# A pre-norm block of splat attention and a gated feed-forward layer: the order of the prologue, of the side work and of the stage loads

## What is computed

```python
x = x + attn(layernorm(x)); x = x + ffn(layernorm(x))
# attn: 16 heads, 16 splats per head, 16 dimensions per head
q, k, v = split(x @ qkv_w.T)
q_weights = exp(sum((q - centers) ** 2) * inv_var)      # per token, head, splat
k_weights = exp(sum((k - centers) ** 2) * inv_var)
logits = einsum('bihs,bjhs,hs->bijh', q_weights, k_weights, amplitudes)
out = softmax(logits / temp, axis=2) @ v ; return out @ out_w.T
# ffn: token shift and gate, x_prev is x moved by one token
xr = mu_r * x + (1 - mu_r) * x_prev ; xk = mu_k * x + (1 - mu_k) * x_prev
return sigmoid(xr @ W_r.T) * (square(relu(xk @ W_k.T)) @ W_v.T)
```

## Time and profile before

| what | us |
|---|---|
| median of 3 runs | 2332.38 (2332.07 to 2335.14) |
| the profiled execution, its own time | 2329.31 |
| its span in the trace | 2327.5 |
| PE busy in the span | 2189.1 (94%) |
| ACT busy in the span | 2003.1 (86%) |
| DVE busy in the span | 907.5 (39%) |
| granted PE clock, mean | 0.984 |

### The profile page before, as it was taken

The page is one execution under the profiler, slowest core; times in us unless marked ns, Lnnn a source line. Parts: engine busy times, 40 slices in busy tenths (PEclk is TensorE's granted clock), DMA queues, the critical chain, the costliest instruction groups (busy, mean ns, idle before and its releaser), DMA issues.

```text
span 2327.5 us, 46042 instructions
## 1 busy us (share of the span) xinstructions
PE 2189.1 (94%) x19886; PEld 902.2 (39%) x19886; DVE 907.5 (39%) x1777; ACT 2003.1 (86%) x2160; POOL 278.4 (12%) x260
## 2 busy tenths in 40 slices
PE   6689999999999899999999999999999999999997
PEld 3233333433443344334444343443433333333344
DVE  4223344334435243452533445244343342323426
ACT  2478999999999799898989999898999999998883
POOL 0112122211110110111102011110200000000000
PEclk9889999999999999999999999999999999999999
DMA  4632425226051421431542243421243131310111
GB/s 131 169 84 87 98 89 119 85 74 155 22 125 56 84 72 47 85 99 37 121 92 82 64 85 99 88 71 45 77 106 76 36 65 47 49 46 17 40 39 35
DMA packets 165582, 180.27 MB, mean 77 GB/s; under 512 B 82832, under 2 KB 108816, under 8 KB 162480
## 3 DMA queue, kind: packets, MB, share of 16 engines
q1 hardware_dynamic: 163264, 177.01, 30.2%
q10 hardware_dynamic: 2096, 0.14, 0.1%
HBM read 86.45 MB, written 75.89 MB: 70 GB/s over the span
## 4 chain that ended last, share of the span: by engine, by line
PE 74%; ACT 16%; DVE 4%; SPq 2%; DMA 2%; issue 1%; ACTq 0%; DVEq 0%
PE ps_pv L700 35%; PE ps_scores L683 21%; ACT probs L1007 14%; PE ps_step L728 13%; PE ps_step L745 2%; PE ps_scores L718 1%; ACT weight L1067 1%; PE ps_scores L713 1%; DVE den_all L1432 1%; SPq L638 1%; DVE o_raw L1317 1%; SPq L510 1%; DMA q_parts<-parts 0%; DMA attn<-attn_kept 0%; DVE mixed_r L1300 0%
## 5 line engine op out<-in xcount | busy, mean ns | idle before, releaser
L1007 ACT ACTIVATE probs<-ps_scores 128x1024 f32<-128x1024 f32 x2048 | 1932.4, 1032 | 226.4 <-PE ps_scores L683 218.8
L700 PE MATMUL ps_pv<-probs,vals 128*32 128x512 f32 x8192 | 1089.5, 616 | 15.4 <-DVE o_raw L1317 12.2
L683 PE MATMUL ps_scores<-q_aug,k_aug 49*128 49x512 f32 x4096 | 722.8, 441 | 42.8 <-ACT probs L1007 36.5
L683 PEld LDWEIGHTS ps_scores<-q_aug,k_aug 49*128 49x128 f32 x4096 | 336.7, 185 | 595.9 <-ACT probs L1007 470.0
L700 PEld LDWEIGHTS ps_pv<-probs,vals 128*32 128x32 f32 x8192 | 255.1, 144 | 347.7 <-issue 277.0
L1124 POOL TENSOR_TENSOR packed<-qk 32x512 f32<-32x512 f32 x224 | 244.7, 1092 | 946.6 <-DVE qk L1250 933.4
L1432 DVE RECIPROCAL den_all<-den_all 128x512 f32<-128x512 f32 x63 | 210.8, 3346 | 0.7
L1129 POOL TENSOR_TENSOR k_act<-k_act 128x512 f32<-128x512 f32 x28 | 30.7, 1096 | 1015.5 <-DVE k_act L1253 1015.5
L1317 DVE COPY o_raw<-ps_pv 128x512 f32<-128x512 f32 x64 | 44.2, 691 | 240.7 <-PE ps_pv L700 240.7
L1250 DVE COPY qk<-ps_step 128x512 f32<-128x512 f32 x56 | 38.7, 691 | 220.4 <-PE ps_step L728 220.4
L1228 DVE TENSOR_SCALAR weight<-ps_step,cen_sq 128x512 f32<-128x512 f32 x57 | 42.8, 750 | 174.6 <-PE ps_step L745 174.5
(11 more groups left out here) (201 smaller groups left out, 1044.5 us busy)
## 6 DMA issues: line engine op xcount, KB each, us to landing
q_aug<-q_parts SPq DMA_DIRECT2D x128, 192.0 KB
k_aug<-k_parts SPq DMA_DIRECT2D x30, 768.0 KB, 10.6
k_parts<-parts SPq DMA_DIRECT2D x32, 512.0 KB, 3.0
q_parts<-parts SPq DMA_DIRECT2D x32, 512.0 KB, 2.8
packed<-qk SPq DMA_DIRECT2D x224, 64.0 KB, 2.0
x_ffn<-x SPq DMA_DIRECT2D x18, 512.0 KB, 4.3
v_kept<-v_rows SPq DMA_DIRECT2D x64, 128.0 KB, 2.4
k_parts<-parts SPq DMA_DIRECT2D x32, 256.0 KB, 3.5
```

The costliest lines, as they stand in the source:

```text
L683: mm = pe.matmul(ps_scores[:, g % RING, e, :], k_aug[rows, s % 2, pair, kt * P:(kt + 1) * P], q_aug[rows, u % 2, pair, :], start=True, sto ...
L700: mm = pe.matmul(ps_pv[32 * c:32 * c + 32, :], vals[:, s % 2, kt, :, c], probs[:, tick % PROB_SLOTS, c, :], start=(kt == 0), stop=(kt == K ...
L1007: act.activation(probs[:, tick % PROB_SLOTS, 2 * pair:2 * pair + 2, :], ps_scores[:, g % RING, :, :], ACT.Exp).then_inc(probs_ready, 1)
```

## The change

The order of work changes; no product, activation or transfer of the steady part is dropped, except that each exponential of weights becomes two, one for each side.

- Prologue: ACT copies tile 0's transposes before it waits for the constants. `q1` is projected before PE waits for the flag, and PE reads the flag only at the end. Values use `v_rows` and `gate` in turn, each with a semaphore. SP stores a tile's values first, then loads the parts and values of the tile before.
- PE's loop: in an odd gap the pieces stand ahead of its one tick of values. An even gap is as before.
- ACT's loop goes by gaps. The weights' exponential is taken per side (128x512), in the first gap of the next four that holds work (`full`), else in the first; the splits and stores follow that.
- `stage_tick` moves a stage's loads out of the nine ticks from an attention load's tick on.
- Two mixing operations that fell on the tick before a unit's end move behind `take`.

```diff
 FIRST = (..., "k1", "value10", "value11",
-         "dist_k0", "dist_q0", "q1", "turn20", "turn21", "k2", ...
+         "q1", "dist_k0", "dist_q0", "turn20", "turn21", "k2", ...
...
+WEIGHED_AFTER = 4
+def gap_of(tick):
+    return next(gap for gap in itertools.count() if name_of(gap) == tick)
+def full(gap):
+    work = PIECES_AT.get(name_of(gap), ())
+    return sum(not name.startswith("turn") for _, name, _ in work) >= (3 if gap % 2 else 1)
+def weigh_gap(task, half, side):
+    first = gap_of(end(task, f"dist_{'kq'[side]}{half}")) + 1
+    if side:
+        first = max(first, weigh_gap(task, half, 0) + 1)
+    return next((gap for gap in range(first, first + WEIGHED_AFTER) if full(gap)), first)
+def split_tick(task, half, side):
+    return name_of(weigh_gap(task, half, side) + 2)
...
 def stage_tick(b, s):
...
-        tick = max([tick] + [end(weighed(b, s, i)[0], f"dist_q{s // 2}") + 10 for i in range(NC)])
+        tick = max([tick] + [split_tick(*weighed(b, s, i), 1) + 4 for i in range(NC)])
...
+    last = KT * FIRST_UNIT[b, s] - 12
+    tick = next((t for t in range(tick, last) if not any(t <= begin(task, "out0") - 5 < t + 9 for task in FFNS)), tick)
...
+def later(tick):
+    return tick + 1 if tick % KT == KT - 2 else tick
...
-DIST_AT = beside((end(task, f"dist_q{half}"), (task, half)) for task, half in WEIGHTS)
+WEIGH_AT = beside((weigh_gap(task, half, side), (task, half, side)) for task, half in WEIGHTS for side in range(2))
+SPLIT_AT = beside((split_tick(task, half, side), (task, half, side)) for task, half in WEIGHTS for side in range(2))
+PARTS_AT = beside((split_tick(task, half, 1) + 2, (task, half)) for task, half in WEIGHTS)
...
-MIX_AT = beside((end(task, "turn1") + (1, 1, 2, 3)[part], (task, part)) ...
-GATE_AT = beside((end(task, name) + 2, (task, name)) ...
+MIX_AT = beside((later(end(task, "turn1") + (1, 1, 2, 3)[part]), (task, part)) ...
+GATE_AT = beside((gap_of(end(task, name)), (task, name)) ...
...
+        first_v = [v_rows, gate]
...
-            for i in range(NC):
-                sp.wait_ge(first_copied, copies_before(f"value{i}1") + 1)
-                store_v(0, i)
+            for i in range(NC + 1):
+                if i < NC:
+                    sp.wait_ge(first_copied, copies_before(f"value{i}1") + 1)
+                    store_v(0, i, first_v[i % 2], first_v_stored[i % 2])
                 if i == 0:
                     sp.wait_ge(setup_dve, SETUP_SHIFT)
                     store_shifts(0, 0)
-                sp.wait_ge(v_stored, 16 * STAGES * (i + 1))
-                load_v(0, 0, TT * i, TT)
-                store_parts(0, i, 0, 2 * i)
-                sp.wait_ge(parts_stored, PARTS * 2 * (i + 1))
-                load_k(0, 0, slice(i * CHUNK, (i + 1) * CHUNK))
-                if i == 0:
-                    sp.wait_ge(shifts_stored, 16)
-                    load_q(0, q_loaded[0])
+                if i:
+                    sp.wait_ge(parts_stored, PARTS * 2 * i)
+                    load_k(0, 0, slice((i - 1) * CHUNK, i * CHUNK))
+                    if i == 1:
+                        sp.wait_ge(shifts_stored, 16)
+                        load_q(0, q_loaded[0])
+                    sp.wait_ge(first_v_stored[(i - 1) % 2], 16 * STAGES * ((i + 1) // 2))
+                    load_v(0, 0, TT * (i - 1), TT)
+                if i < NC:
+                    store_parts(0, i, 0, 2 * i)
...
+            first_project("q", 1)
             pe.wait_ge(setup_dve, SETUP_STEPS)
-            unsafe = pe.value_load(flag[0:1, 0:1], min_val=0, max_val=1)
             first_distance("k", 0)
             first_distance("q", 0)
-            first_project("q", 1)
...
                 ticks = values_in(gap)
-                for tick in ticks[:1]:
+                for tick in ticks[:-1]:
                     values(tick)
                 for task, name, part in PIECES_AT.get(name_of(gap), ()):
...
-                for tick in ticks[1:]:
+                for tick in ticks[-1:]:
                     values(tick)
...
             def first_values(i):
-                if i:
-                    act.wait_ge(v_stored, 16 * STAGES * i)
+                if i >= 2:
+                    act.wait_ge(first_v_stored[i % 2], 16 * STAGES * (i // 2))
...
+            first_turned(0)
             act.wait_ge(consts_loaded, 16 * N_CONSTS)
...
-            first_turned(0)
...
+            for gap in range(GAPS):
+                for g in range(3 * gap, min(3 * gap + 3, 2 * TICKS)):
+                    exponentials(g)
...
+                for task, half, side in WEIGH_AT.get(gap, ()):
+                    act.wait_ge(step_free, STEP_NO[task, f"dist_{'kq'[side]}{half}"] + 1)
+                    act.activation(weight[:, side, :], weight[:, side, :], ACT.Exp, scale=inv_var[:, half:half + 1]).then_inc(weighted, 1)
```

More of the change, by code:

```diff
@@ L242, in queries_tick @@
     if which:
-        tick = max(tick, end(which[0], f"dist_q{which[1]}") + 9)
+        tick = max(tick, split_tick(*which, 1) + 3)
     assert tick < KT * u - 5, (u, tick)
@@ L601, in _ @@
                     store_attn(u)
-                for task, half in DIST_AT.get(tick - 7, ()):
+                for task, half in PARTS_AT.get(tick, ()):
                     store_parts(task[1], task[2], half, PARTS_BEFORE[task, half])
@@ L1060, in _ @@
             first_weights(3)
-            for tick in range(EVENT_TICKS):
-                if tick < TICKS:
-                    exponentials(2 * tick)
-                for task, half in DIST_AT.get(tick - 4, ()):
-                    act.wait_ge(step_free, STEP_NO[task, f"dist_q{half}"] + 1)
-                    act.activation(weight[:, :, :], weight[:, :, :], ACT.Exp, scale=inv_var[:, half:half + 1]).then_inc(weighted, 1)
-                if tick < TICKS:
-                    exponentials(2 * tick + 1)
-                for task, name in GATE_AT.get(tick, ()):
+            for gap in range(GAPS):
+                for g in range(3 * gap, min(3 * gap + 3, 2 * TICKS)):
+                    exponentials(g)
+                for task, name in GATE_AT.get(gap, ()):
                     two = slice(2 * int(name[1]), 2 * int(name[1]) + 2)
@@ L1450, in _ @@
                     layernorm("ffn", n, x_ffn[:, n % 2, :, :], h_ffn, ffn_ln, part)
-                for task, half in DIST_AT.get(tick - 5, ()):
-                    late_split(task, half, 0)
-                for task, half in DIST_AT.get(tick - 6, ()):
-                    late_split(task, half, 1)
+                for task, half, side in SPLIT_AT.get(tick, ()):
+                    late_split(task, half, side)
             u = UNITS - 1
```

26 lines of the change are left out of this document (16 added, 10 removed).

## The result

The changed kernel takes 2279.97 us (median of 4 runs, 2277.29 to 2282.12), the kernel before 2333.03 in the same session (4 runs). The ratio is 0.9773, 95% interval 0.9761 to 0.9786: faster by 53 us. The forecast was 2282, range 2264 to 2303. The profiled execution took 2282.12 us, its span is 2280.3 (before: 2329.31 and 2327.5).

The account below looks back on a forecast made before the run. PE's order was taken to set the time (PE busy 94%, ACT 86%). The terms summed to -50.1 us against the profiled 2329.3, giving 2279.2; the median counterpart, 3.1 higher, was 2282, range 2264 to 2303.

Parts of the forecast that it names:

- three signs of being wrong: Stop for `packed` ending past 112 us, odd gaps staying at 3.21 us, or PE's waits for DVE passing 20 us.
- Term 1: Prologue and first stop: PE's restart moves with SP's earlier entry into the loop; -15.6 us.
- Term 2: Loop, attention loads: issuing them ahead of the stage's loads removes PE's two stops and the half clock after; -15.5 us.
- Term 3: PE's odd gaps: pieces ahead of values shorten a full gap from 3.21 to 3.14 us; -11 us.
- Term 4: ACT's weights' exponentials by sides: two of three places where PE idled and fell to half clock go; -6 us.
- Term 5: DVE's queue: earlier splits and two mixing operations behind `take` save 1 us each in some four places; -4 us.
- term 6: Odd gaps: values no longer cover a first piece's wait, and `take` has only the scores as cover; +2 us.
- The rival in which it moves on to something waited for: SP's hold behind stage loads falls on something waited for; attention loads gain 0, total 2298 us; chance 0.08.
- all boundaries cost alike: PE's odd gaps: order of scores, pieces and values is worth nothing, total 2293 us; chance 0.15.
- The slower rival: Steps starting in odd gaps wait uncovered for DVE or DMA; 2406 us if all 135 wait; chance 0.03.

## Why the prediction was right

The total came within 2 us of the median, and that is in part luck, as the terms show. None of the three signs of being wrong appeared, though one was near: the stop ended at 111.31 us (wrong past 112, forecast 107.5), odd gaps went to 3.18, and PE's waits for DVE from 125 to 2200 us were 14.6 us. By its terms (against the profiled executions):

| term | forecast | measured | from |
|---|---|---|---|
| 1 prologue and stop | -15.6 | -12.0 | restart |
| 2 attention loads | -15.5 | -15.6 | the two pairs |
| 3 pieces ahead of values | -11 | -8.2 | put back, in the trace (9.7 without the pair at 1539 us) |
| 4 exponentials by sides | -6 | -12 | put back: 10.2 + 2.2; 11.8 beside term 3, from gap 14 |
| 5 DVE's queue | -4 | at most -1.5 of its own | what is left |
| 6 lost cover | +2 | +0.5 | a wait of 0.51 us for `gate_in`, pair at 889 us |
| tail | none | +4.6 | same code |

Errors of both signs cancelled. The account by stretches closes: 12.0 to the restart, 2.7 to gap 14 (term 4's first pair and its neighbours), then 15.6 for the attention loads, 20.0 for terms 3 and 4 together and 1.5 for the rest, less 4.6 in the tail, are 47.2.

**Term 1** had the mechanism right, that the restart moves with SP's entry and not with PE's start. The head gained 4.6 us where I said 4.0, `k3` and the third split stood within 0.8 us of what I walked, the third landing at 73.14 (said 73.6). The step that failed is the fourth tile's: "only the split, issue and landing remain: 6.9 us, so 80.5". It landed at 83.52, 3.0 us late, and both parts of the way grew. From the split at 73.03 to the end of the last issue are 5.0 us, against 3.8 for the third tile before, and from there to the landing 5.5 us, against 3.0 before and with SP's old order. And "the change alters none of these rows" was 1 us off: entry to restart is 19.1 us, not 18.05. The stop did not shrink to 13 us, since PE's first scores came as early as forecast and the restart did not. The claim that the second buffer and SP's order each do their part was not tested by the walk: the runs show that either does nearly all.

**Term 2** is right in size and kind; the held issue moved to a store with slack, as the written order said. The rival in which it moves on to something waited for falls.

**Term 3** had the sign right and the size too large. The failing step is "0.89 + 1.28 + 0.97 = 3.14": the pieces take 1.32 from their start to the values', so the way from pieces to values costs 0.04 too, and the gain is 0.03 a gap and not 0.07. The count was too small in turn, as gaps with fewer pieces gain as much. The Trainium skill (TensorE: Matmul & The Clock Gate, Part 3: Packing small matmuls) says that a weight load overlaps matmuls in flight only where the row groups differ; that all boundaries cost alike was what I made of it, and it would have given nothing. The run that puts the order back is 8 us slower. Nor does the trace agree with the Trainium skill's statement: in the odd gap above the values' first weights load at 431.40 us, 0.2 us ahead of the first values at 431.61 and just as the last four instructions of the pieces start, and both kinds use all 128 rows (timeline of PE's weight loads):

```profile
431.40 0.37 PEld L742 LDWEIGHTS ps_pv<-probs,vals 128*32 128x32 f32 x8
```

The first weights of a block of scores load only as it starts, and so do those of the pieces behind scores. Both orders have one boundary with such an early load in an odd gap, so this doesn't tell why they differ by 0.03 us; that stays open.

**Term 4** was too small by half. "12 pairs stood in gaps with four pieces per pair already and cost nothing there" was the wrong step: eight of these pairs lasted 6.68 to 6.76 us in the trace of before, where a full pair lasts 6.42, and last 6.40 to 6.43 now; I had looked only at pairs with a stop. The other part had the mechanism right: the pairs at gaps 10, 30 and 68 went from 9.48, 9.48 and 8.32 to 7.26, 7.46 and 6.64, 5.9 us. The 6 us forecast came about by two errors: the loss was 5.9 us and not 8.8, as repaired pairs there last 6.6 to 7.5 us, and I counted two of three places where all three lost their half clock. Gap 68 is also at full clock with the exponential whole, so its 1.7 us are not shown to be this term's. Of the 12.4 us that the reversed kernel gives back, 4.2 are the pairs at gaps 10 and 30, 2.2 the eight pairs, and 3.2 the half clock at gaps 42 and 94, which before had not; 1.5 of the rest stand at two pairs where PE waits longer for DVE.

On the Trainium skill's budget (ScalarE: Activation LUTs, Rules for kernel authors) of about 0.3 us for each activation: the records of the weights' exponentials in the loop seem to agree (56 of 0.752 us against 28 of 1.160, 9.6 us more), but records of neighbouring activations overlap. (So do the two copies in the earlier trace rows that I read as the price of two activations.) ACT's busy time on the page is 2005.4 us against 2002.6 with the exponentials whole, 0.1 us for each of the 28, and the time went down.

**Term 5** has little of its own. The mixing part showed no effect. Of what `take` gained (12.2 to 9.6 us), 1.0 comes with the pieces ahead of the values (10.6 with values first). Another 1.0 goes only when exponentials, splits and gate are put back as well (11.6); put back alone they leave it at 9.6. In the pair at 789.4 us, which holds a unit's first values, the new order gained 1.0 us where term 6 had looked for lost cover.

**The slower rival** (cover lost everywhere) did not show, since DVE is early at steps that start in odd gaps. It is real in even gaps, as the run with all values last shows.

## What to carry to other kernels

When one queue issues everything in order, look at what its held issue is and who waits behind it; moving a big load behind small ones that are waited for brought the restart 12.9 us forward here, for one number. Two fixes for one wait are worth one: put each back alone, and then both, before counting them. To price a small edit, compare the same stretch of two traces block by block; the medians of runs here carry 5 us of head and tail that no edit made.

## What the runs showed of the hardware that I had not expected

- Behind the loads of a stage (two of 768 KB and one of values) SP's next issue, where it follows at once, takes 10.3 to 15.5 us in the fourteen traces, whatever it is (queries, `x_ffn`, a store); without them ahead the same issue took 0.31 us. The hold runs from the loads and not from the next issue: one that comes 3 us behind them takes 9.4 to 9.5 us, one 12 us behind or later 0.3 to 0.6.
- A stop of PE costs more than its length: rows at half clock for 20 us around the 17.73 us stop, 7 us around the 4.73 us stop, none without one. But waits of 0.4 us in a row can end at half clock too (gap 42), and whether they do differs from kernel to kernel and, at head, tail and the pair at 1539 us, with identical code.
- The order of blocks on PE changes the spacing by 0.03 us a gap with the same instructions.
